# Two tiles in turn for the raw rotary rows, and a softmax that works in place in the probability tiles

## The chip, the cores and the metric

The kernel runs on one core of a Trainium2 chip. The metric is the device time of one execution in microseconds (us). Five engines work at the same time, each through its own list of instructions in order: PE (TensorE, matrix products into PSUM), DVE (VectorE), ACT (ScalarE), POOL (GpSimd) and SP, which here only issues DMAs. They are tied to each other by semaphores: an instruction can wait until a counter has reached a value, and raises another when it is done.

## The reference, cut to what matters

One transformer layer on `x` of 64 sequences, 64 tokens, 512 features: a conditioning product, latent attention with rotary positions, a residual, then a product with a per-sequence adapter and a mixture of four experts. The change touches the attention alone:

```python
h = x @ WA + bA                                   # x here is the conditioned input
kv_lat, q_lat = jnp.split(h, 2, axis=-1)
kRt = _rope(h @ WB + bB, 0)                       # 64 rotary key features, shared by the heads
qRt = _rope(h @ WC + bC, 0)                       # 16 heads x 64 rotary query features
...
scores = jnp.einsum('bhqd,bhkd->bhqk', qf, kf) * dk ** (-0.5)
scores = jnp.where(causal, scores, -jnp.inf)
attn = jax.nn.softmax(scores, axis=-1)
```

`_rope(x)` is `x * cos + rot * sin`, where `rot` swaps the two features of each pair, with a minus sign on the first.

## The kernel before, in words

`absorb_weights` prepares products of weights, `attention` follows, then `routing` and `experts`. In the profile the attention fills the time from 47 us to about 1000 us. It goes through 8 groups g of 8 sequences, each 512 tokens wide. The code is written out by hand for each engine: a part `first` for the start of group 0, and a `body` that is looped over the groups and holds the rest of group g together with the start of group g+1. The order inside an engine's list is the order of the source; nothing is reordered.

**The rotary chain.** The rotary features stand in nine blocks of 128x512 a group: one of keys and eight of queries, u = 0 to 7. A block passes through four engines:

- PE writes the product into one of two PSUM banks, `bank_p[u % 2]` (three matmuls for each of two halves of the latent, L95 to L97).
- ACT adds the bias and writes the block to the tile `raw` (`keys_raw` L500, `q_raw` L507). The profile calls the tile rope_raw.
- POOL multiplies `raw` by the cosines into `q_rope` (`q_cos` L424; for keys `keys_cos` L416, twice as long, into `kblk`).
- DVE (`turn` L629) issues a one-element memset that only carries waits (L633), swaps the pairs of `raw` into `swapped` (shuffle L634) and multiplies by the sines (L638). Then `queries_rope` adds the result to `q_rope` (L657), or `keys_rope` adds it to `kblk` (two halves, L649).

There is one `raw`. ACT may write block u only when DVE has swapped and POOL has multiplied the block before it (waits on `swap_ev` and `cos_ev`, L505 and L506). PE uses a bank again only when ACT has emptied it (`raw_ev`, L851 and L859).

The chain runs twice for each group. I call the two places **the front** (blocks keys, 0, 1, 2, 3 of group g+1, written into the end of group g's body) and **the middle** (blocks 4 to 7 of group g, in the first third of its body). PE's list there is as follows, with Q(u) the product of block u, wz the output projection of an attention step into `bank_o`, and KA(h) the absorbed keys of head h:

- front: Q0, wz, Q1, wz, Q2, wz, Q3, wz, KA0, KA1, then the first product of wz of step 6. KA0 waits for block 2 to be in `raw`, KA1 for block 3.
- middle: Q4, two wz, Q5, two wz, Q6, two wz, Q7, two wz, a transpose, KA8, KA9, mix of step 2, then the first product of wz of step 1. KA8 waits for block 6, KA9 for block 7.

The wz of a step overwrites `bank_o`, so its first product waits for `x2_ev` (L921): DVE must have added the last result to the residual rows (`x2_tile`, L699). The places of `x2_tile` in DVE's list matter below. In the middle it is queries_rope(4), the sum of step 3, queries_rope(5), queries_rope(6), **x2_tile(0)**, queries_rope(7). In the front it is keys_rope, queries_rope(0), queries_rope(1), **x2_tile(5)**, queries_rope(2), queries_rope(3).

POOL's list in the middle is cosines 4, cosines 5, `gated` of step 3 (L431, which waits for DVE's reciprocal), `residual_bias` (L437), cosines 6, cosines 7. In the front it is the keys' cosines, then 0 to 3. ACT's list holds the copies to `raw` in a row, behind the exponential of step 3 in the middle.

**The softmax.** Each group has 8 steps. `less_max` on DVE scales and masks the scores from PSUM into `score` (L675), takes the maximum (L680) and subtracts it (L682); ACT takes the exponential of `score` into `prob[i % 2]` (L516); `softmax_sum` sums it (L688), and POOL multiplies `prob` by the reciprocal (L431). Step n of `less_max` waits for the exponential of step n-1 (`exp_ev`), as there is one `score`. The sum of step n-1, which waits for that same exponential, stands ahead of it in DVE's list in every case.

Of the kernel before, what the change touches and what calls it, by code (L numbers as in the profile page):

```python
# [26 lines left out]
ALU = mybir.AluOpType  # L27
ACT = mybir.ActivationFunctionType
AX = mybir.AxisListType.X
# [285 lines left out]
def attention(nc, K, A, W, out):  # L315

    with ExitStack() as ctx:
        def sb(name, shape, dt=F32):
            return ctx.enter_context(nc.sbuf_tensor(name, shape, dt))
# [19 lines left out]
        lat_h, lat_l = sb("lat_h", [P, 2, GT], F32R), sb("lat_l", [P, 2, GT], F32R)  # L339
        kv_tok = sb("kv_tok", [P, GB, L])  # L340
        q_rope = sb("q_rope", [P, UB, GT])
        raw, swapped = sb("rope_raw", [P, GT]), sb("rope_swapped", [P, GT])
        lat_bias = (raw, swapped)
        bias_sel = swapped[0:NSUB, :].rearrange("n (b d) -> n b d", b=GB)
        score = sb("score", [P, HB, C])
        prob = sb("prob", [P, 2, HB, C])
        rmax, rsum, rinv = sb("rmax", [P, HB]), sb("rsum", [P, HB]), sb("rinv", [P, HB])
        wait_here = sb("wait_here", [1, 1])
# [56 lines left out]
        @block.gpsimd  # L405
        def _(pool):
            def bias_rows(g):
                pool.wait_ge(S["rope_done"], g * NR)
                nc.gpsimd.tensor_tensor(bias_sel[:, :, :],
                                        K["sel"][:, bass.ds(g * GB, GB)].unsqueeze(2).to_broadcast([NSUB, GB, C]),  # L410
                                        K["fside"][:, :].unsqueeze(1).to_broadcast([NSUB, GB, C]),
                                        ALU.mult).then_inc(S["bias_sel_ready"], 1)

            def keys_cos(g):
                pool.wait_ge(S["raw_ev"], g * NR + 1)
                nc.gpsimd.tensor_tensor(kblk[:, :, :, :],  # L416
                                        raw[:, :].rearrange("p (b t) -> p b t", b=GB).unsqueeze(2).to_broadcast([P, GB, 2, C]),
                                        K.parts["cosk"].rearrange("p (h t) -> p h t", h=2).unsqueeze(1).to_broadcast(
                                            [P, GB, 2, C]), ALU.mult).then_inc(S["cos_ev"], 1)

            def q_cos(g, u):
                pool.wait_ge(S["raw_ev"], g * NR + u + 2)
                cos = K.parts["cosq"][:, u * C:(u + 1) * C]
                nc.gpsimd.tensor_tensor(q_rope[:, u % UB, :].rearrange("p (b t) -> p b t", b=GB),  # L424
                                        raw[:, :].rearrange("p (b t) -> p b t", b=GB),
                                        cos.unsqueeze(1).to_broadcast([P, GB, C]), ALU.mult).then_inc(S["cos_ev"], 1)


            def gated(g, i):
                pool.wait_ge(S["inv_ev"], g * STEPS + i + 1)  # L430
                nc.gpsimd.tensor_tensor(prob[:, i % 2, :, :], prob[:, i % 2, :, :],  # L431
                                        rinv[:, :].unsqueeze(2).to_broadcast([P, HB, C]),
                                        ALU.mult).then_inc(S["prob_ev"], 1)

            def residual_bias(g, t):
                pool.wait_ge(xres_in[t], g * 16 + 16)
                nc.gpsimd.tensor_tensor(x_res[:, t, :], x_res[:, t, :], K["bZ"][:, :],  # L437
                                        ALU.add).then_inc(S["xres_biased"], 1)

            def project_front(g):  # L440
                keys_cos(g)
                for u in range(UB):
                    q_cos(g, u)

            def first():
                bias_rows(0)
                project_front(0)
                gated(0, 0)
                gated(0, 1)

            def body(g, more):
                gated(g, 2)
                residual_bias(g, 0)
                q_cos(g, 4)
                q_cos(g, 5)
                gated(g, 3)
                residual_bias(g, 1)
                q_cos(g, 6)
                q_cos(g, 7)
                residual_bias(g, 2)  # L460
                gated(g, 4)
                if more:
                    bias_rows(g + 1)
                residual_bias(g, 3)
                gated(g, 5)
                gated(g, 6)
                gated(g, 7)
                if more:
                    project_front(g + 1)
                    gated(g + 1, 0)  # L470
                    gated(g + 1, 1)

            over_groups(pool, first, body)

        @block.scalar
        def _(act):
# [20 lines left out]
            def keys_raw(g):  # L497
                act.wait_ge(S["lat_ev"], g * 2 + 2)
                act.wait_ge(S["keys_mm"], g + 1)
                nc.scalar.activation(raw[:, :], bank_p[1][:, :], ACT.Identity, bias=K["bB"][:, 0:1]  # L500
                                     ).then_inc(S["raw_ev"], 1)

            def q_raw(g, u):
                act.wait_ge(S["qr_mm"], g * NU + u + 1)
                act.wait_ge(S["swap_ev"], g * NR + u + 1)  # L505
                act.wait_ge(S["cos_ev"], g * NR + u + 1)  # L506
                nc.scalar.activation(raw[:, :], bank_p[u % 2][:, :], ACT.Identity, bias=K["bC"][:, u:u + 1]  # L507
                                     ).then_inc(S["raw_ev"], 1)

            def keys_absorbed(g, h):  # L510
# [2 lines left out]

            def exps(g, i):
                act.wait_ge(S["sub_ev"], g * STEPS + i + 1)
                nc.scalar.activation(prob[:, i % 2, :, :], score[:, :, :], ACT.Exp).then_inc(S["exp_ev"], 1)  # L516

            def prob_transposed(g, i):
                act.wait_ge(S["pt_mm"], g * STEPS + i + 1)
# [87 lines left out]
        def _(dve):  # L607
# [18 lines left out]
                nc.vector.tensor_tensor(lat_l[:, i, :], lat32[i], lat_h[:, i, :].bitcast(F32),  # L626
                                        ALU.subtract).then_inc(S["lat_lo"], 1)

            def turn(r, sin):  # L629

                dve.wait_ge(S["raw_ev"], r + 1)
                dve.wait_ge(S["rope_done"], r)
                nc.vector.memset(wait_here[:, :], 0.0)  # L633
                nc.vector.stream_shuffle(swapped[:, :], raw[:, :], [i ^ 1 for i in range(32)]  # L634
                                         ).then_inc(S["swap_ev"], 1)
                dve.wait_ge(S["swap_ev"], r + 1)
                v = swapped[:, :].rearrange("p (b t) -> p b t", b=GB)
                nc.vector.tensor_tensor(v, v, sin.unsqueeze(1).to_broadcast([P, GB, C]), ALU.mult  # L638
                                        ).then_inc(S["sin_ev"], 1)
                dve.wait_ge(S["sin_ev"], r + 1)  # L640

            def keys_rope(g):
                r = g * NR
                dve.wait_ge(S["lat_ev"], g * 2 + 2)
                turn(r, K.parts["sink"])
                dve.wait_ge(S["cos_ev"], r + 1)
                for h in range(2):
                    rows = slice(h * DR, (h + 1) * DR)
                    last = nc.vector.tensor_tensor(kblk[rows, :, h, :], kblk[rows, :, h, :],  # L649
                                                   swapped[rows, :].rearrange("p (b t) -> p b t", b=GB), ALU.add)  # L650
                last.then_inc(S["rope_done"], 1)

            def queries_rope(g, u):
                r = g * NR + 1 + u
                turn(r, K.parts["sinq"][:, u * C:(u + 1) * C])
                dve.wait_ge(S["cos_ev"], r + 1)
                nc.vector.tensor_tensor(q_rope[:, u % UB, :], q_rope[:, u % UB, :], swapped[:, :], ALU.add  # L657
                                        ).then_inc(S["rope_done"], 1)
# [8 lines left out]
            def per_head(row):  # L667
                return row[:, :].unsqueeze(2).to_broadcast([P, HB, C])

            def less_max(g, i, first=False):  # L670
                n = g * STEPS + i + 1
                dve.wait_ge(S["s_mm"], n)
                if not first:
                    dve.wait_ge(S["exp_ev"], n - 1)
                nc.vector.scalar_tensor_tensor(out=score[:, :, :],  # L675
                                               in0=bank_s[i % 2][:, :].rearrange("p (h t) -> p h t", h=HB), scalar=SCALE,
                                               in1=K.parts["mask"].unsqueeze(1).to_broadcast([P, HB, C]),
                                               op0=ALU.mult, op1=ALU.add).then_inc(S["score_ev"], 1)
                dve.wait_ge(S["score_ev"], n)
                nc.vector.tensor_reduce(rmax[:, :], score[:, :, :], AX, ALU.max).then_inc(S["max_ev"], 1)  # L680
                dve.wait_ge(S["max_ev"], n)
                nc.vector.tensor_tensor(score[:, :, :], score[:, :, :], per_head(rmax),  # L682
                                        ALU.subtract).then_inc(S["sub_ev"], 1)

            def softmax_sum(g, i, first=False):
                n = g * STEPS + i + 1
# [21 lines left out]
            def first():  # L708
# [7 lines left out]
                keys_rope(0)  # L716
                for u in range(UB):
                    queries_rope(0, u)
                less_max(0, 0, first=True)
                softmax_sum(0, 0, first=True)  # L720
                less_max(0, 1)
                softmax_sum(0, 1)
# [1310 lines left out]
```

## Time and profile before

| | us |
|---|---|
| median of 3 runs | 1977.47 |
| lowest and highest of the runs | 1977.43 and 1979.97 |
| the profiled execution, its time | 1983.41 |
| the profiled execution, its span (first to last instruction) | 1981.5 |
| of the span: PE busy | 1849.3 |
| of the span: DVE, POOL, ACT busy | 927.4, 716.0, 627.8 |

The durations used below come from the profiled execution. Its time is 1.9 us more than its span and 5.9 us more than the median of the runs. A group is what lies between one KA9 and the next, some 115 to 117 us. The granted clock is the share of TensorE's full 2.4 GHz that the chip gave: 1.00 is full speed and 0.50 is 1.2 GHz.

### The profile page before, as it was taken

To read this page: it belongs to the slowest core of one execution; us is meant where nothing else is said; L and a number is where in the kernel's file an instruction comes from. 1 tells how busy PE (TensorE), PEld (TensorE's weight loads), DVE (VectorE), ACT (ScalarE), POOL (GpSimd) and SP (SyncE) were. 2 spreads that over 40 slices of the span, in tenths; PEclk is the share of its full clock that TensorE was granted. 3 is DMA by queue.
4 is the path that set the end of the run, shared out by engine and by line. 5 is a ranking of instruction groups with operands and counts; after the bars stand their busy time and mean duration, and the time that the engine had idled before them with its cause. 6 is when DMAs were issued, how large, how long until landed. Compare 5 with 4: busy or idle time off the path is not lost. (4 is left out here: it accounts for less than half of the span.)

```text
span 1981.5 us, 26865 instructions
## 1 busy us (share of the span) xinstructions
PE 1849.3 (93%) x9384; PEld 1434.4 (72%) x9384; DVE 927.4 (47%) x1589; ACT 627.8 (32%) x1088; POOL 716.0 (36%) x524
## 2 busy tenths in 40 slices
PE   6799999999999999999979997999999999999996
PEld 4577676767777676767767775878787878787875
DVE  4566656656665665666422585233323232223321
ACT  4333333333333333333223212333333333333331
POOL 1232222223221222322100013666656574757563
PEclk9999999999999999999989997999999999999998
DMA  7000101001010100101043214223303330422011
GB/s 251 22 1 17 48 5 58 0 26 37 16 48 5 58 0 26 37 16 48 11 111 106 75 64 145 79 41 127 65 21 81 110 64 0 123 89 42 2 20 22
DMA packets 69028, 104.88 MB, mean 53 GB/s; under 512 B 12288, under 2 KB 29440, under 8 KB 68992
## 3 DMA queue, kind: packets, MB, share of 16 engines
q1 hardware_dynamic: 49408, 77.70, 11.8%
q0 software_dynamic: 7168, 16.78, 4.6%
q10 hardware_dynamic: 12416, 9.92, 1.6%
q8 instruction: 23, 0.38, 0.1%
q14 instruction: 13, 0.11, 0.0%
HBM read 79.21 MB, written 25.17 MB: 53 GB/s over the span
## 5 line engine op out<-in xcount | busy, mean ns | idle before, releaser
L1843 DVE CAST hh<-hid 128x512 fp32r<-128x512 f32 x128 | 77.3, 604 | 474.7 <-ACT hid L1788 474.5
L1718 POOL TENSOR_TENSOR w1l<-w_raw,w1h 128x512 fp32r<-128x512 f32 x112 | 179.5, 1603 | 163.6 <-ACT w1h L1780 151.7
L431 POOL TENSOR_TENSOR prob<-prob,rinv 128x512 f32<-128x512 f32 x64 | 66.7, 1043 | 469.6 <-DVE rinv L692 469.6
L95 PE MATMUL e_h<-xh,w1h 128*128 (+1 forms) x512 | 202.8, 396 | 14.7 <-POOL w1l L1718 13.3
L95 PE MATMUL bank_o<-Mh,mix_h 128*128 128x512 f32 x512 | 213.3, 417 | 2.3 <-DVE mix_l L663 1.4
L97 PE MATMUL bank_o<-Mh,mix_l 128*128 128x512 f32 x512 | 203.8, 398 | 0.0
L96 PE MATMUL bank_o<-Ml,mix_h 128*128 128x512 f32 x512 | 203.5, 397 | 0.0
L95 PE MATMUL e_y<-w2h,hh 128*128 128x512 f32 x512 | 200.3, 391 | 1.6 <-DVE hl L1845 1.6
L96 PE MATMUL e_h<-xl,w1h 128*128 (+1 forms) x512 | 201.4, 393 | 0.0
L97 PE MATMUL e_h<-xh,w1l 128*128 (+1 forms) x512 | 201.2, 393 | 0.0
L97 PE MATMUL e_y<-w2h,hl 128*128 128x512 f32 x512 | 199.4, 389 | 0.0
L96 PE MATMUL e_y<-w2l,hh 128*128 128x512 f32 x512 | 199.3, 389 | 0.0
L1723 POOL TENSOR_TENSOR w2l<-w_raw,w2h 128x512 fp32r<-128x512 f32 x112 | 151.0, 1348 | 52.3 <-ACT w2h L1784 52.3
L1788 ACT ACTIVATE hid<-e_h 128x512 f32<-128x512 f32 x128 | 76.7, 599 | 264.7 <-PE e_h L97 264.7
L424 POOL TENSOR_TENSOR q_rope<-rope_raw,table_attend 128x512 f32<-128x512 f32 x64 | 102.6, 1603 | 80.4 <-ACT rope_raw L507 80.4
L1784 ACT CAST w2h<-w_raw 128x512 fp32r<-128x512 f32 x112 | 69.7, 622 | 179.9 <-PE e_y L97 179.9
L95 PEld LDWEIGHTS e_h<-xh,w1h 128*128 128x128 f32 x512 | 97.3, 190 | 38.1 <-POOL w1l L1718 16.3
L95 PEld LDWEIGHTS bank_o<-Mh,mix_h 128*128 128x128 f32 x512 | 97.9, 191 | 30.9 <-issue 10.7
L97 PEld LDWEIGHTS bank_o<-Mh,mix_l 128*128 128x128 f32 x512 | 97.4, 190 | 23.3
L95 PEld LDWEIGHTS e_y<-w2h,hh 128*128 128x128 f32 x512 | 96.1, 188 | 22.9 <-DVE hl L1845 3.3
L97 PEld LDWEIGHTS e_h<-xh,w1l 128*128 128x128 f32 x512 | 97.3, 190 | 20.5
L96 PEld LDWEIGHTS bank_o<-Ml,mix_h 128*128 128x128 f32 x512 | 98.3, 192 | 19.0
(278 smaller groups left out, 3561.3 us busy)
## 6 DMA issues: line engine op xcount, KB each, us to landing
w_raw<-in_W_dram SPq DMA_DIRECT2D x56, 512.0 KB, 4.2
stage<-in_x_dram SPq DMA_DIRECT2D x8, 1024.0 KB, 6.3
x_res<-in_x_dram SPq DMA_DIRECT2D x32, 256.0 KB, 2.7
out_dram<-x_res SPq DMA_DIRECT2D x32, 256.0 KB, 2.0
flat_dram<-flat_sb ACTq DMA_DIRECT2D x32, 256.0 KB, 2.0
rows<-out_dram SPq DMA_DIRECT2D x4, 1024.0 KB, 5.1
x_odd<-out_dram SPq DMA_DIRECT2D x4, 1024.0 KB, 6.0
stage<-in_W_dram SPq DMA_DIRECT2D x8, 512.0 KB, 5.8
```

Source lines behind the costliest of these rows:

```text
L95: nc.tensor.matmul(out, ah, bh, start=start and n == 0, stop=False)
L96: nc.tensor.matmul(out, ah, bl, start=False, stop=False)
L97: last = nc.tensor.matmul(out, al, bh, start=False, stop=stop and n == len(pairs) - 1)
L424: nc.gpsimd.tensor_tensor(q_rope[:, u % UB, :].rearrange("p (b t) -> p b t", b=GB), raw[:, :].rearrange("p (b t) -> p b t", b=GB), cos.uns ...
L431: nc.gpsimd.tensor_tensor(prob[:, i % 2, :, :], prob[:, i % 2, :, :], rinv[:, :].unsqueeze(2).to_broadcast([P, HB, C]), ALU.mult).then_inc ...
L1718: nc.gpsimd.tensor_tensor(w1l[:, k, :, :], w1_at(pair, chunk), w1h[:, k, :, :].bitcast(F32), ALU.subtract).then_inc(S["w1_lo"], 1)
L1723: nc.gpsimd.tensor_tensor(w2l[:, k, :], w2_at(pair, chunk), w2h[:, k, :].bitcast(F32), ALU.subtract).then_inc(S["w2_lo"], 1)
L1784: nc.scalar.copy(w2h[:, k, :], w2_at(pair, chunk)).then_inc(S["w2_hi"], 1)
L1788: nc.scalar.activation(hid[:, k, :], bank_h[k][:, :], ACT.Gelu).then_inc(S["h_act"], 1)
L1843: nc.vector.tensor_copy(hh[:, k, :], hid[:, k, :]).then_inc(S["h_hi"], 1)
```

## The change

`raw` becomes two tiles. Block u of the queries uses `raw[u % 2]`, and the keys use `raw[1]`. ACT's copy of block u now waits for the swap and the cosines of the block two before it, and the copy of block 0 has no such wait at all. `score` is gone: `less_max` writes its three results to the half of `prob` that the exponential then overwrites in place, and no longer waits for `exp_ev`. The tiles together take the same space. Every engine's list holds the same work in the same order as before; only waits and the tiles read and written differ.

```diff
-        raw, swapped = sb("rope_raw", [P, GT]), sb("rope_swapped", [P, GT])
-        lat_bias = (raw, swapped)
+        raw = [sb(f"rope_raw{k}", [P, GT]) for k in range(2)]
+        swapped = sb("rope_swapped", [P, GT])
+        lat_bias = (raw[0], swapped)
...
-        score = sb("score", [P, HB, C])
...
             def keys_raw(g):
                 act.wait_ge(S["lat_ev"], g * 2 + 2)
                 act.wait_ge(S["keys_mm"], g + 1)
-                nc.scalar.activation(raw[:, :], bank_p[1][:, :], ACT.Identity, bias=K["bB"][:, 0:1]
+                nc.scalar.activation(raw[1][:, :], bank_p[1][:, :], ACT.Identity, bias=K["bB"][:, 0:1]
...
             def q_raw(g, u):
                 act.wait_ge(S["qr_mm"], g * NU + u + 1)
-                act.wait_ge(S["swap_ev"], g * NR + u + 1)
-                act.wait_ge(S["cos_ev"], g * NR + u + 1)
-                nc.scalar.activation(raw[:, :], bank_p[u % 2][:, :], ACT.Identity, bias=K["bC"][:, u:u + 1]
+                if u:
+                    act.wait_ge(S["swap_ev"], g * NR + u)
+                    act.wait_ge(S["cos_ev"], g * NR + u)
+                nc.scalar.activation(raw[u % 2][:, :], bank_p[u % 2][:, :], ACT.Identity, bias=K["bC"][:, u:u + 1]
...
-                nc.scalar.activation(prob[:, i % 2, :, :], score[:, :, :], ACT.Exp).then_inc(S["exp_ev"], 1)
+                nc.scalar.activation(prob[:, i % 2, :, :], prob[:, i % 2, :, :], ACT.Exp).then_inc(S["exp_ev"], 1)
...
+                row = prob[:, i % 2, :, :]
                 dve.wait_ge(S["s_mm"], n)
-                if not first:
-                    dve.wait_ge(S["exp_ev"], n - 1)
-                nc.vector.scalar_tensor_tensor(out=score[:, :, :],
-                                               in0=bank_s[i % 2][:, :].rearrange("p (h t) -> p h t", h=HB), scalar=SCALE,
+                nc.vector.scalar_tensor_tensor(out=row, in0=bank_s[i % 2][:, :].rearrange("p (h t) -> p h t", h=HB),
...
-                nc.vector.tensor_reduce(rmax[:, :], score[:, :, :], AX, ALU.max).then_inc(S["max_ev"], 1)
+                nc.vector.tensor_reduce(rmax[:, :], row, AX, ALU.max).then_inc(S["max_ev"], 1)
...
-                nc.vector.tensor_tensor(score[:, :, :], score[:, :, :], per_head(rmax),
-                                        ALU.subtract).then_inc(S["sub_ev"], 1)
+                nc.vector.tensor_tensor(row, row, per_head(rmax), ALU.subtract).then_inc(S["sub_ev"], 1)
```

The shuffle in `turn` and the two cosine products read `raw[1]` or `raw[u % 2]` in the same way.

## Rows read from the trace of the kernel before

**Rows 1.** The page's first part: busy us, share of the span, instructions.

```profile
PE 1849.3 (93%) x9384; PEld 1434.4 (72%) x9384; DVE 927.4 (47%) x1589; ACT 627.8 (32%) x1088; POOL 716.0 (36%) x524
```

**Rows 2.** PE's waits, whole span: us in total, times, longest us.

```profile
PE bank_p L95 <- ACT rope_raw L507: 42.7, 32, 2.2
```

**Rows 3.** Timeline, middle of group 1: start, us, operation xcount [idle before <-releaser].

```profile
224.84 1.30 POOL L424 TENSOR_TENSOR q_rope<-rope_raw,table_attend 128x512 f32<-128x512 f32 x1 [3.54 <-ACT rope_raw L507]
...
225.73 0.96 DVE L638 TENSOR_TENSOR rope_swapped<-rope_swapped,table_attend 128x512 f32<-128x512 f32 x1
...
226.72 0.69 DVE L657 TENSOR_TENSOR q_rope<-q_rope,rope_swapped 128x512 f32<-128x512 f32 x1
...
227.00 1.57 POOL L424 TENSOR_TENSOR q_rope<-rope_raw,table_attend 128x512 f32<-128x512 f32 x1 [0.86 <-ACT rope_raw L507]
...
228.28 0.74 DVE L634 STREAM_SHUFFLE rope_swapped<-rope_raw 128x512 f32<-128x512 f32 x1
...
229.54 1.73 POOL L437 TENSOR_TENSOR x_res<-x_res,bZ 128x512 f32<-128x512 f32 x1
```

**Rows 4.** The timeline goes on, up to the first wz of step 1.

```profile
230.16 1.66 DVE L657 TENSOR_TENSOR q_rope<-q_rope,rope_swapped 128x512 f32<-128x512 f32 x1
...
231.23 1.71 POOL L424 TENSOR_TENSOR q_rope<-rope_raw,table_attend 128x512 f32<-128x512 f32 x1
...
233.77 0.50 PE L95 MATMUL bank_p<-lat_h,Ah 128*128 128x512 f32 x1 [1.94 <-ACT rope_raw L507]
...
234.13 0.68 DVE L699 TENSOR_TENSOR x_res<-bank_o,x_res 128x512 f32<-128x512 f32 x1
...
235.73 0.50 PE L95 MATMUL bank_o<-Mh,mix_h 128*128 128x512 f32 x1
```

**Rows 5.** Timeline, front of group 2.

```profile
293.00 2.21 DVE L638 TENSOR_TENSOR rope_swapped<-rope_swapped,table_attend 128x512 f32<-128x512 f32 x1
...
295.24 2.39 DVE L649 TENSOR_TENSOR k_blocks<-k_blocks,rope_swapped 64x512 f32<-64x512 f32 x2
...
295.50 1.57 POOL L424 TENSOR_TENSOR q_rope<-rope_raw,table_attend 128x512 f32<-128x512 f32 x1 [0.86 <-ACT rope_raw L507]
...
298.65 0.69 ACT L507 ACTIVATE rope_raw<-bank_p,bC 128x512 f32<-128x512 f32 x1 [3.23 <-DVE rope_swapped L634]
...
299.38 0.69 DVE L657 TENSOR_TENSOR q_rope<-q_rope,rope_swapped 128x512 f32<-128x512 f32 x1
...
300.24 0.75 DVE L634 STREAM_SHUFFLE rope_swapped<-rope_raw 128x512 f32<-128x512 f32 x1
...
302.42 0.68 DVE L699 TENSOR_TENSOR x_res<-bank_o,x_res 128x512 f32<-128x512 f32 x1
...
304.52 0.50 PE L95 MATMUL bank_p<-lat_h,Ah 128*128 128x512 f32 x1 [1.50 <-ACT rope_raw L507]
```

**Rows 6.** Timeline, PE in the front of group 1: KA1 and what follows it.

```profile
189.24 0.51 PE L95 MATMUL bank_p<-lat_h,Ah 128*128 128x512 f32 x1 [0.88 <-ACT rope_raw L507]
...
190.05 0.39 PE L95 MATMUL bank_o<-Mh,mix_h 128*128 128x512 f32 x1
```

**Rows 7.** Timeline, end of the attention: a wz product that waits for `x2_tile`.

```profile
974.13 0.69 DVE L699 TENSOR_TENSOR x_res<-bank_o,x_res 128x512 f32<-128x512 f32 x1 [2.22 <-PE bank_o L97]
...
974.97 0.48 PE L95 MATMUL bank_o<-Mh,mix_h 128*128 128x512 f32 x1 [0.44 <-DVE x_res L699]
```

**Rows 8.** Timeline, PE in the front of group 0: its KA1.

```profile
78.81 0.50 PE L95 MATMUL bank_p<-lat_h,Ah 128*128 128x512 f32 x1 [1.45 <-ACT rope_raw L507]
```

**Rows 9.** Busy us (instructions) by stretch; after POOL the granted clock, DMA share, GB/s.

```profile
117.20:120.40 3.20, 3.20 (x11) 1.69 (x10) 3.13 (x6) 1.42 (x4) 2.24 (x2) 0.50 0.01 3
305.00:308.20 3.20, 3.20 (x9) 2.46 (x8) 2.42 (x6) 0.59 (x1) 1.34 (x1) 0.50 0.24 74
233.77:350.57 116.80, 111.28 (x617) 82.63 (x617) 71.06 (x128) 38.85 (x68) 29.94 (x22) 0.99 0.08 27
350.57:465.74 115.17, 109.65 (x616) 81.49 (x616) 71.08 (x128) 38.83 (x68) 29.97 (x22) 1.00 0.08 27
```

More of the change, by code:

```diff
@@ L416, in keys_cos @@
                 nc.gpsimd.tensor_tensor(kblk[:, :, :, :],
-                                        raw[:, :].rearrange("p (b t) -> p b t", b=GB).unsqueeze(2).to_broadcast([P, GB, 2, C]),
+                                        raw[1][:, :].rearrange("p (b t) -> p b t", b=GB).unsqueeze(2).to_broadcast([P, GB, 2, C]),
                                         K.parts["cosk"].rearrange("p (h t) -> p h t", h=2).unsqueeze(1).to_broadcast(
@@ L424, in q_cos @@
                 nc.gpsimd.tensor_tensor(q_rope[:, u % UB, :].rearrange("p (b t) -> p b t", b=GB),
-                                        raw[:, :].rearrange("p (b t) -> p b t", b=GB),
+                                        raw[u % 2][:, :].rearrange("p (b t) -> p b t", b=GB),
                                         cos.unsqueeze(1).to_broadcast([P, GB, C]), ALU.mult).then_inc(S["cos_ev"], 1)
@@ L627, in latent_lo, with turn @@
                                         ALU.subtract).then_inc(S["lat_lo"], 1)
-            def turn(r, sin):
+            def turn(r, k, sin):
                 dve.wait_ge(S["raw_ev"], r + 1)
@@ L633, in turn @@
                 nc.vector.memset(wait_here[:, :], 0.0)
-                nc.vector.stream_shuffle(swapped[:, :], raw[:, :], [i ^ 1 for i in range(32)]
+                nc.vector.stream_shuffle(swapped[:, :], raw[k][:, :], [i ^ 1 for i in range(32)]
                                          ).then_inc(S["swap_ev"], 1)
@@ L644, in keys_rope @@
                 dve.wait_ge(S["lat_ev"], g * 2 + 2)
-                turn(r, K.parts["sink"])
+                turn(r, 1, K.parts["sink"])
                 dve.wait_ge(S["cos_ev"], r + 1)
@@ L654, in queries_rope @@
                 r = g * NR + 1 + u
-                turn(r, K.parts["sinq"][:, u * C:(u + 1) * C])
+                turn(r, u % 2, K.parts["sinq"][:, u * C:(u + 1) * C])
                 dve.wait_ge(S["cos_ev"], r + 1)
@@ L668, in per_head, with less_max @@
                 return row[:, :].unsqueeze(2).to_broadcast([P, HB, C])
-            def less_max(g, i, first=False):
+            def less_max(g, i):
                 n = g * STEPS + i + 1
+                row = prob[:, i % 2, :, :]
                 dve.wait_ge(S["s_mm"], n)
-                if not first:
-                    dve.wait_ge(S["exp_ev"], n - 1)
-                nc.vector.scalar_tensor_tensor(out=score[:, :, :],
-                                               in0=bank_s[i % 2][:, :].rearrange("p (h t) -> p h t", h=HB), scalar=SCALE,
-                                               in1=K.parts["mask"].unsqueeze(1).to_broadcast([P, HB, C]),
+                nc.vector.scalar_tensor_tensor(out=row, in0=bank_s[i % 2][:, :].rearrange("p (h t) -> p h t", h=HB),
+                                               scalar=SCALE, in1=K.parts["mask"].unsqueeze(1).to_broadcast([P, HB, C]),
                                                op0=ALU.mult, op1=ALU.add).then_inc(S["score_ev"], 1)
                 dve.wait_ge(S["score_ev"], n)
-                nc.vector.tensor_reduce(rmax[:, :], score[:, :, :], AX, ALU.max).then_inc(S["max_ev"], 1)
+                nc.vector.tensor_reduce(rmax[:, :], row, AX, ALU.max).then_inc(S["max_ev"], 1)
                 dve.wait_ge(S["max_ev"], n)
-                nc.vector.tensor_tensor(score[:, :, :], score[:, :, :], per_head(rmax),
-                                        ALU.subtract).then_inc(S["sub_ev"], 1)
+                nc.vector.tensor_tensor(row, row, per_head(rmax), ALU.subtract).then_inc(S["sub_ev"], 1)
             def softmax_sum(g, i, first=False):
@@ L718, in first @@
                     queries_rope(0, u)
-                less_max(0, 0, first=True)
+                less_max(0, 0)
                 softmax_sum(0, 0, first=True)
```

## The prediction

> **What bounds the kernel now.** I read the busy shares first: PE is busy 93% of the span and no other engine over half [rows 1]. So the time is PE's list, and the change can only alter the waits in it. The list of waits by engine comes next. The largest wait of PE is for ACT's copy to the raw rotary tile, 42.7 us in 32 waits [rows 2]. The softmax does not appear among PE's waits. The timeline then shows who makes each copy late. In the middle, KA9 has stood still for 1.94 us for block 7 [rows 4]. In the front, the copy of block 1 starts at 298.65, released by DVE's shuffle, and KA1 is held for 1.50 us [rows 5]. What the reader should look for in these rows is how long the same operation takes. L638, L657 and L649 on DVE read two SBUF tiles and take 0.69 us when POOL is quiet, but 0.96, 1.66 and 2.21 us when POOL is at work [rows 3 to 5].
>
> **How DVE and POOL block each other.** Block 4's cosines end at 226.14 and L638, begun during them, ends at 226.69, which is 0.55 later. The bias row L437 ends at 231.27 and L657, begun during it, ends at 231.82, again 0.55 later [rows 3, 4]. So DVE's two-input operation stands until POOL's ends. The other way round, the cosines begun at 231.23 end 1.12 after L657, and those begun at 227.00 end 1.16 after it, against 1.30 for an undisturbed one [rows 3, 4]. My two rules for this kernel are thus: **blocked DVE operation ends 0.55 after POOL's, blocked POOL cosine or bias operation ends 1.15 after DVE's**, and the one already waiting goes ahead of the one issued later. L437 was waiting at 229.54, and L657 at 230.16 had to let it pass [rows 3, 4].
>
> **The removed wait of the softmax.** It costs nothing today: the sum of step n-1 stands ahead of `less_max(n)` in DVE's list and waits for the same exponential. In place or not, the instructions have the same sizes. I put this part at 0; a few tens of ns in 64 steps on an engine with slack would not reach PE either way.
>
> **The middle, worked through.** ACT can now copy block 5 right behind block 4 (ready about 225.5, one copy of 0.69 after the start of block 4's cosines), block 6 as soon as its product is there, and block 7 after the shuffle of block 5. Block 4's steps up to 226.69 stay. Then:
> - POOL no longer waits for block 5. It has been ready since 226.14, goes next, and its cosines end at 226.69 + 1.15 = 227.84. Before, they began at 227.00, after L657 had got in [rows 3].
> - L657 of block 4 is therefore blocked and ends at 228.39 instead of 227.41: 0.98 lost.
> - Block 5's shuffle began 0.87 after L657's end [rows 3], so now at 229.26, ending at 230.00. The copy of block 7 is done at 230.7. KA9, which could follow KA8 at 231.8 (233.77 less 1.94), has **no wait left**: 1.94 us gained.
> - L437 began 2.13 after that L657's end, as `gated` ended [rows 3], so now at 230.52. L638 of block 5 ends at 231.10, L437 at 232.25, L657 of block 5 at 232.80.
> - Block 6: cosines end at 233.95, L638 at 234.50. Before, block 7's cosines came after L657 of block 6. Now block 7 is ready and waiting, so they go first, until 235.65, and L657 of block 6 ends at 236.20: once more 1 us lost.
> - x2_tile(0) stands behind it and starts 0.08 before its end, at 236.12 instead of 234.13 [rows 4].
> - The first wz of step 1 may start 0.84 after x2_tile's start [rows 7]: **236.96 instead of 235.73** [rows 4]. PE would be there at 233.8 (235.73 less 1.94) and stands for some 3.2 us.
>
> So each middle loses 1.23 us: the wait for block 7 is replaced by a longer one for x2_tile(0). Eight middles: **+9.8 us**. From below, with POOL's earlier cosines costing DVE nothing, x2_tile stays at 234.13, wz starts at 234.97, and a middle gains 0.76.
>
> **The front, worked through.** Keys' L638 ends at 295.21 [rows 5]. Block 0 is ready by then, as nothing holds its copy, and its cosines end at 296.36. The first half of L649 ends at 296.91, block 1's cosines at 298.06, the second half at 298.61 instead of 297.63 [rows 5]. The copy that block 0's shuffle released began 1.02 after L649 [rows 5]. Now that is block 2's, so it runs from 299.63 to 300.32. L657 of block 0 ended 2.44 after L649 [rows 5]: 301.05. Block 2's cosines end at 302.20, L638 of block 1 at 302.75. Block 1's shuffle ended 3.36 after L649 [rows 5], so the copy of block 3 is done 4.08 after it, at 302.69. KA1 starts at 302.74 instead of 304.52. Before, wz came 0.81 after KA1 [rows 6], nominally at 305.33. Now it also needs x2_tile(5), behind L657 of block 1. That L657 is issued at 302.79, and block 3's cosines at 302.77. The two are within 0.03:
> - POOL first: cosines until 304.07, L657 until 304.62, x2_tile from 304.54, wz at 305.38: **0.0 gained**.
> - DVE first: L657 until 303.48, x2_tile from 303.40, wz at 304.24: **1.09 gained**.
> - From below, with no new blocking: copy of block 3 after the shuffle's end at 300.99, KA1 at 301.76, x2_tile as before at 302.42, wz at 303.26, 2.07 gained.
>
> I take the first, since POOL's request is the earlier one. Seven fronts: **0.0 us**, ends 0 and -14.5. On this tie the Trainium skill says (SBUF — State Buffer, Who interferes with whom) that issue order decides who blocks. That names POOL by the order worked out above; a wrong order of 0.03 would move the sum by 7 x 1.09 = 7.6 us. The front of group 0 has no x2_tile. Its KA1 moves like the other, by 302.74 - 304.52 = -1.78, from 78.81 [rows 8]: **-1.8 us**.
>
> **The clock.** After a stall the granted clock is at 0.50 for a stretch. This follows 3 of the 8 middles (first: 117.2) and 5 of the 7 fronts (first of full cost: 305.0) [rows 9]. A group with one such stretch takes 116.80, one with none 115.17 [rows 9]: **1.6 us each**. A front has some 3.3 us of waits within 7 us. The new middle has about 3.2 us in one piece, so I give it the front's share: 8 x 5/7 = 5.7 stretches instead of 3, +2.7 x 1.6 = **+4.4 us**. The ends are 0 and, with all fifteen places hit, 7 x 1.6 = +11.2.
>
> **Sum.** 9.8 + 0.0 - 1.8 + 4.4 = +12.4 us on the profiled execution (1983.4 to 1995.8, span 1981.5 to 1993.9). On the median of the runs it gives 1977.5 + 12.4 = **1990 us**. Behind the two places nothing else that the change delays is waited for soon: blocks 2 and 3 of a front are needed by the next group's scores, behind six more KA and six wz products, and block 7 of a middle by step 4's scores, later still.
>
> **Rivals.**
> - *DVE first in the fronts.* For it: L657 has won by 0.04 elsewhere. Against: here it is second. 12.4 - 7.6 = +4.8, **1982 us**.
> - *Double buffering pays.* The new tile takes DVE's and POOL's turns off the chain without new blocking: 7 x -2.07, 8 x -0.76, and the first front at -2.7 (78.81 to 76.1) make -23.3, and up to four stretches of low clock fewer -6.4; between them **1951 us**. For it: PE waits 42.7 us for this tile [rows 2]. Against: DVE's list is already full from the first shuffle on, and POOL's turns move onto it. It decides the case if POOL's cosines do not get in ahead of L657.
> - *The clock falls at every place.* 9.8 - 1.8 + 11.2 = +19.2, **1997 us**. For it: a middle's wait grows from 1.9 to 3.2 us. The Trainium skill warns of this (TensorE: Matmul & The Clock Gate, HAM oscillation): a wait that recurs in each tile makes the engine pay the clock's step each time. No row here has a single attention stall of that length, so the chance rests on the fronts.
> - *Nothing moves.* Gains of fronts and losses of middles cancel, without more low clock: 9.8 - 7.6 - 1.8 = +0.4, **1978 us**.
>
> **How the numbers follow.** Chances: forecast 0.40, DVE first 0.20, pays 0.17, clock at every place 0.15, nothing 0.08. "Faster" and "slower" mean by over 0.2% (4 us), about what can be told from no change: faster 0.17. Same takes the last and the lower half of DVE first, 0.18; slower is the rest, 0.65. The range runs from just below "nothing moves" to just above the clock rival, 1975 to 2000, and leaves "pays" out.
>
> **What would show it.** In the timeline of the middle: block 5's cosines start as block 4's end, L657 of block 4 takes 1.7 instead of 0.69, KA9 has no wait, and the first wz of step 1 waits about 3.2 us for x2_tile. In PE's waits: the 42.7 us fall to about 20, and a new row for x_res L699 has 25 us (8 x 3.2) plus up to 13 (7 x 1.8). The distance of one KA9 to the next grows by 1.2 us, or 1.2 plus a multiple of 1.6. I am wrong if L657 of block 4 still takes 0.69, or if wz waits for something else.

## The result, and the profile after

| | before | changed |
|---|---|---|
| median, us | 1977.47 (1976.43 to 1984.36, 5 runs) | 1991.51 (1989.88 to 1992.95, 4 runs) |
| ratio to before | | 1.0061, 95% interval 1.0045 to 1.0078 |
| again, beside the experiments below | 1980.02 (17 runs) | 1991.51 (6 runs), ratio 1.0053, 1.0040 to 1.0066 |
| profiled execution: time, span | 1983.41, 1981.5 | 1989.88, 1987.9 |

The changed kernel is slower by 0.5 to 0.6%, 11.5 to 14 us. One more execution of it took 2104.89 us at a mean granted clock of 0.84, where the others had 0.97, and is left out. The two profiled executions are only 6.5 us apart, because that of before is one of its longer ones. Later readings therefore use stretches that can be compared, not the two spans.

PE's waits in the changed kernel, whole span (total us, times, longest); the first rows answer to [rows 2]:

```profile
PE bank_o L95 <- DVE x_res L697: 26.2, 14, 3.2
PE bank_p L95 <- ACT rope_raw L508: 19.5, 17, 2.8
```

The 42.7 us for the raw tile have become 19.5, and a wait of 26.2 us for `x2_tile` has appeared. Before, PE waited 0.9 us for `x2_tile`, in two places at the end of the attention. So the sum of the two rows went from 43.6 to 45.7, 2 us more. That alone does not explain 11.5 us or more.

The middle of group 1 in the timeline, answering to [rows 3, 4]. L639 and L658 are before's L638 and L657, L697 is its L699:

```profile
221.98 2.99 POOL L424 TENSOR_TENSOR q_rope<-rope_raw,table_attend 128x512 f32<-128x512 f32 x2 [3.54 <-ACT rope_raw L508]
...
222.86 0.96 DVE L639 TENSOR_TENSOR rope_swapped<-rope_swapped,table_attend 128x512 f32<-128x512 f32 x1
...
223.85 1.67 DVE L658 TENSOR_TENSOR q_rope<-q_rope,rope_swapped 128x512 f32<-128x512 f32 x1
...
226.43 1.04 POOL L431 TENSOR_TENSOR prob<-prob,rinv 128x512 f32<-128x512 f32 x1 [1.47 <-DVE rinv L690]
227.43 1.75 POOL L437 TENSOR_TENSOR x_res<-x_res,bZ 128x512 f32<-128x512 f32 x1
...
228.06 1.67 DVE L658 TENSOR_TENSOR q_rope<-q_rope,rope_swapped 128x512 f32<-128x512 f32 x1
...
229.14 3.40 POOL L424 TENSOR_TENSOR q_rope<-rope_raw,table_attend 128x512 f32<-128x512 f32 x2
...
231.44 1.64 DVE L658 TENSOR_TENSOR q_rope<-q_rope,rope_swapped 128x512 f32<-128x512 f32 x1
...
233.01 0.68 DVE L697 TENSOR_TENSOR x_res<-bank_o,x_res 128x512 f32<-128x512 f32 x1
...
233.83 0.77 PE L95 MATMUL bank_o<-Mh,mix_h 128*128 128x512 f32 x1 [3.15 <-DVE x_res L697]
```

POOL's cosines now run in pairs (x2, 2.99 and 3.40 us), and each second one falls on an L658: the adds of blocks 4 and 6 (223.85 and 231.44) take 1.67 and 1.64 us where 0.69 stood before. The add of block 5 (228.06) was blocked before too, 1.66 us. DVE reaches `x2_tile(0)` late, and PE stands for 3.15 us.

The front of group 2, answering to [rows 5]:

```profile
295.88 3.37 DVE L650 TENSOR_TENSOR k_blocks<-k_blocks,rope_swapped 64x512 f32<-64x512 f32 x2
...
303.42 0.69 DVE L658 TENSOR_TENSOR q_rope<-q_rope,rope_swapped 128x512 f32<-128x512 f32 x1
...
303.46 1.79 POOL L424 TENSOR_TENSOR q_rope<-rope_raw,table_attend 128x512 f32<-128x512 f32 x1 [0.69 <-ACT rope_raw L508]
```

PE in the same front:

```profile
290.47 0.40 PE L95 MATMUL bank_p<-lat_h,WBh 128*128 128x512 f32 x1
...
300.97 0.50 PE L95 MATMUL bank_p<-lat_h,Ah 128*128 128x512 f32 x1 [0.61 <-ACT rope_raw L508]
...
303.44 0.50 PE L95 MATMUL bank_p<-lat_h,Ah 128*128 128x512 f32 x1 [1.50 <-ACT rope_raw L508]
...
304.86 0.47 PE L95 MATMUL bank_o<-Mh,mix_h 128*128 128x512 f32 x1 [0.46 <-DVE x_res L697]
```

The keys' adds (L650, before's L649) take 3.37 instead of 2.39. Of the near tie, DVE won by 0.04 (303.42 against 303.46), so `x2_tile(5)` is hardly late: 0.46 us of wait.

**A measure for a group.** From the first matmul of the keys' block in one front to that in the next, PE's work is the same in both kernels. The rows are of the kind of [rows 9]: the stretch, its length, the busy time (and count) of PE, PEld, DVE, ACT and POOL, then the granted clock, the DMA share and GB/s. First before: six groups in one piece, then one group alone.

```profile
174.22:873.55 699.33, 666.97 (x3697) 495.04 (x3696) 426.44 (x763) 233.01 (x403) 179.69 (x132) 0.99 0.08 27
406.57:521.75 115.18, 109.66 (x617) 81.49 (x616) 71.09 (x128) 38.85 (x68) 29.97 (x22) 1.00 0.08 27
```

And for the changed kernel, six groups and then the longest kind of group:

```profile
172.52:878.16 705.64, 671.23 (x3698) 500.42 (x3696) 436.54 (x763) 233.80 (x403) 185.66 (x132) 0.97 0.08 27
407.17:525.95 118.78, 113.42 (x617) 84.39 (x616) 72.75 (x128) 38.96 (x68) 30.95 (x22) 0.96 0.08 26
```

A group at full clock took 115.18 us before; its mean over six was 116.56 (699.33 / 6). The changed kernel's mean is 117.61, and its clock over the six groups is 0.97 instead of 0.99. It has no group at full clock: the first takes 117.95 us, and the others alternate between 116.7 and 118.8. So the traces alone do not say how much of the 1.05 us a group is wait and how much is clock. The experiments below separate them.

### The profile page after: what moved, and what is told of

Read it like the earlier page. It is cut to its first block and busy times, and to the rows that moved or that the text cites. A ratio compares the mean times of both kernels' runs of the same rounds, so it can differ in the third digit from the quotient of the medians.

```text
span 1987.9 us, 26787 instructions
## 1 busy us (share of the span) xinstructions
PE 1855.8 (93%) x9384; PEld 1443.2 (73%) x9384; DVE 934.6 (47%) x1589; ACT 629.2 (32%) x1088; POOL 724.5 (36%) x524
## 5 line engine op out<-in xcount | busy, mean ns | idle before, releaser
L1841 DVE CAST hh<-hid 128x512 fp32r<-128x512 f32 x128 | 71.8, 561 | 482.9 <-ACT hid L1786 482.9
L95 PE MATMUL bank_o<-Mh,mix_h 128*128 128x512 f32 x512 | 215.0, 420 | 27.7 <-DVE x_res L697 26.2
L424 POOL TENSOR_TENSOR q_rope<-rope_raw,table_attend 128x512 f32<-128x512 f32 x64 | 107.2, 1689 | 50.7 <-ACT rope_raw L508 50.6
L96 PEld LDWEIGHTS e_h<-xl,w1h 128*128 128x128 f32 x512 | 98.2, 192 | 20.3
```

Of the source, the lines that this page charges most:

```text
L95: nc.tensor.matmul(out, ah, bh, start=start and n == 0, stop=False)
L96: nc.tensor.matmul(out, ah, bl, start=False, stop=False)
L1841: nc.vector.tensor_copy(hh[:, k, :], hid[:, k, :]).then_inc(S["h_hi"], 1)
```

## The experiments

I call **the port** whatever it is that DVE's two-input operations and POOL's operations share. The rows show it only by its effect, that one stands until the other ends.

Theory: the rotary copies are early enough now, but POOL's earlier cosines keep DVE from the port, `x2_tile(0)` is late, and after the longer wait the clock is low. Rivals: the in-place softmax costs something; the fronts lose, not the middles; the wait counts and the clock does not. Each line of the table stands against 1979.8 to 1980.1 us of the kernel before, which ran beside them. "Six groups" is the measure above, from each kernel's profile. The last column is the mean granted clock over all executions of that kernel; the kernel before has 0.975 to 0.976. What it is worth can be estimated from two executions of the kernel before, 1976.85 us at 0.978 and 1985.69 us at 0.972: about 1.5 us for each 0.001.

| kernel | median, us | ratio, 95% interval | six groups, us | clock |
|---|---|---|---|---|
| in place only | 1980.05 | 0.9999 (0.9988 to 1.0009) | 699.02 | 0.976 |
| double in middles only | 1988.80 | 1.0047 (1.0033 to 1.0061) | 704.35 | 0.974 |
| double in fronts only | 1976.09 | 0.9987 (0.9978 to 0.9996) | 693.18 | 0.973 |
| changed, POOL held in middles | 1976.17 | 0.9981 (0.9972 to 0.9990) | 697.01 | 0.968 |
| changed, x2_tile earlier | 1955.39 | 0.9866 (0.9851 to 0.9881) | 678.69 | 0.974 |
| before, x2_tile earlier | 1981.22 | 1.0009 (0.9997 to 1.0021) | 700.11 | 0.975 |
| changed, x2_tile earlier, POOL held everywhere | 1962.55 | 0.9905 (0.9891 to 0.9920) | 683.42 | 0.971 |
| changed again | 1991.51 | 1.0053 (1.0040 to 1.0066) | 707.07 | 0.967 |
| changed, middles filled | 1979.68 | 0.9997 (0.9988 to 1.0006) | 695.55 | 0.974 |
| changed, middles and fronts filled | 1971.34 | 0.9954 (0.9939 to 0.9969) | 691.56 | 0.981 |
| changed, x2_tile earlier, fronts filled | 1948.21 | 0.9836 (0.9821 to 0.9851) | 672.03 | 0.979 |
| before, fronts filled | 1978.60 | 0.9996 (0.9987 to 1.0005) | 696.56 | 0.976 |

**The softmax in place alone.** The kernel before, with `score` replaced by the rows of `prob` and without the wait for `exp_ev`, as in the diff of the change.

> The kernel before with the softmax in place alone: no score tile, no wait for the exponential, one raw rotary tile as before. Port theory (all of the loss comes from POOL's cosines getting ahead of L657): as before, 1977 us within 3 us, PE waits 42 to 43 us for the raw tile. Rival, that the softmax in place costs something: part or all of the 14 us, 1982 to 1991 us, and the exponential or the three DVE steps of a softmax longer than their 0.63 and 0.69 us.

Measured 1980.05 us, ratio 0.9999. PE's wait for the raw tile is 43.9 us in 33 waits. The grouped rows of ACT and of DVE in this kernel, 93 to 910 us (busy us, mean ns of one | idle before):

```profile
L515 ACT ACTIVATE prob<-prob 128x512 f32<-128x512 f32 x57 | 36.0, 632 | 96.6 <-DVE prob L679 95.9
...
L679 DVE TENSOR_TENSOR prob<-prob,rmax 128x512 f32<-128x512 f32 x57 | 39.4, 692 | 2.0
```

The exponential takes 632 ns and the subtraction 692 ns, as before. This part of the change is worth nothing in time. It gives the space of `score` to the second raw tile.

**The two places apart.** In the changed kernel, the copies of one place wait for the block just before, as they did before the change:

```diff
             def q_raw(g, u):
                 act.wait_ge(S["qr_mm"], g * NU + u + 1)
-                if u:
-                    act.wait_ge(S["swap_ev"], g * NR + u)
-                    act.wait_ge(S["cos_ev"], g * NR + u)
+                back = 0 if u >= UB else 1
+                act.wait_ge(S["swap_ev"], g * NR + u + back)
+                act.wait_ge(S["cos_ev"], g * NR + u + back)
```

> The changed kernel, but in the fronts (blocks 0 to 3) ACT waits for the block just before, as it did before the change; only the middles use the two tiles in turn. Port theory: the first wz of step 1 waits 3.15 us for x2_tile(0) in each middle as in the changed kernel, and the fronts are those of before, so the fronts' gain of some 1 us each is gone: 1991.5 + 8 = 1999 us, at least 1993. Rival, that the loss sits in the fronts: 1977 us or less.

The kernel for the fronts has 0 and 1 the other way round, and keeps `if u:`, so that the copy of block 0 has no such wait.

> The changed kernel, but in the middles (blocks 4 to 7) ACT waits for the block just before; only the fronts use the two tiles in turn. Port theory: middles as before (KA9 waits 1.94 us, no wait for x2_tile(0)), fronts about 1 us shorter each: 1977.5 - 1.8 - 7 = 1969 us. Rival, that the loss sits in the fronts or in anything both places share: 1985 us or more.

Measured 1988.8 and 1976.1 us. The signs are the theory's and against the rival: middles lose, fronts gain. The sizes are not. The fronts were to give 8 to 9 us against before (1969) and give 3.7; the middles were to cost 13 to 19 and cost 9. A group of the middles-only kernel at full clock, then a group of the fronts-only kernel with one stretch at 0.50:

```profile
413.21:529.37 116.16, 109.53 (x617) 81.49 (x616) 71.83 (x128) 38.94 (x68) 30.75 (x22) 1.00 0.08 27
```

```profile
233.08:348.82 115.74, 111.06 (x616) 82.63 (x616) 71.92 (x128) 38.82 (x68) 30.20 (x22) 0.99 0.08 27
```

The first is 0.98 us longer than before's 115.18, and that is the pure price of a middle. The second, less 1.6 for its stretch, is 114.1: 1.0 less, the pure gain of a front.

The clock explains the sizes in part. Eight middles at 0.98 are 7.8 of the 9 us. The expectation had added what the changed kernel loses by its clock, and in this kernel little of that is there: the six groups hold 7.4 us of it (704.35 - 6 x 116.16), before's hold 8.2 (699.33 - 6 x 115.18), although each of its middles has the wait of 3.15 us. In the fronts-only kernel the six groups are 6.2 us shorter than before's, but the medians differ by only 3.7. The profiled execution of before is 3.6 us above the median of 1979.8 and this one is at its median, and the mean clock is 0.973 against 0.975, some 3 us by the estimate above. So a part of the fronts' gain went to the clock; the runs do not show how much more closely than that.

**POOL held back in the middles.** In the changed kernel, one wait more:

```diff
             def q_cos(g, u):
                 pool.wait_ge(S["raw_ev"], g * NR + u + 2)
+                if u in (5, 7):
+                    pool.wait_ge(S["rope_done"], g * NR + u + 1)
```

> The changed kernel with one wait more on POOL: the cosines of blocks 5 and 7 start only when DVE has added block 4 and block 6. ACT's copies are as early as in the changed kernel. Port theory: L657 of blocks 4 and 6 is back at 0.69 us, x2_tile(0) comes 2 us earlier, the wait for it falls from 3.15 to about 1.2 us in each middle; 8 x 2 = 16 us less, 1975 us, or 1970 with fewer stretches of low clock. Rival, that the loss has another cause than the order at the port: 1991 us or more, since the edit only adds a wait.

Measured 1976.17 us, 15 us less by a wait that was only added. The middle of group 1 in this kernel (L660 is the add, L426 the cosines, L699 x2_tile):

```profile
222.64 0.69 DVE L660 TENSOR_TENSOR q_rope<-q_rope,rope_swapped 128x512 f32<-128x512 f32 x1
...
223.48 1.29 POOL L426 TENSOR_TENSOR q_rope<-rope_raw,table_attend 128x512 f32<-128x512 f32 x1 [1.42 <-DVE q_rope L660]
...
229.73 0.69 DVE L660 TENSOR_TENSOR q_rope<-q_rope,rope_swapped 128x512 f32<-128x512 f32 x1
```

PE at the end of that middle:

```profile
231.17 0.51 PE L95 MATMUL bank_o<-Mh,mix_h 128*128 128x512 f32 x1 [1.71 <-DVE x_res L699]
```

The adds of blocks 4 and 6 are back at 0.69, and the wait for `x2_tile(0)` has fallen from 3.15 to 1.71 (1.2 was expected). The order at the port is shown as the cause of the lateness. The clock has hardly a part in these 15 us: its mean is 0.968, and 0.967 in the changed kernel.

**x2_tile(0) one place earlier.** In DVE's list of the changed kernel, and then of the kernel before:

```diff
                 queries_rope(g, 5)
-                queries_rope(g, 6)
                 x2_tile(g, 0)
+                queries_rope(g, 6)
                 queries_rope(g, 7)
```

> The changed kernel with x2_tile(0) one place earlier in DVE's list, ahead of queries_rope(6). Port theory with the wait for x2_tile as the price: the 3.15 us in front of the first wz of step 1 are gone in the seven looped middles and 1.5 us in the last, 23.5 us less, and the stretches of low clock behind the middles with them (up to 8 x 1.6 us): 1958 to 1968 us. L657 of block 4 still takes 1.67 us. Rival, that the clock or the timing of later stages made the difference: 1985 us or more.

> The kernel before with the same move of x2_tile(0). With one raw tile the copy of block 7 waits for the shuffle of block 6, which x2_tile now pushes 0.7 us back, past the end of its cosines: KA9 waits some 0.4 us longer, 8 x 0.4 = 3 us more, 1980 us. So the move helps only where the raw tile is doubled. Rival, that the place of x2_tile was a flaw in itself: 1970 us or less.

Measured 1955.39 and 1981.22 us. With two raw tiles the move is worth 36 us against the changed kernel, and ends 3 us below the range expected; with one it is worth nothing. In the first kernel the add of block 4 still takes 1.67 us and PE waits nowhere in the middles. The two edits need each other: one takes away PE's wait for block 7, the other its wait for x2_tile(0). A part of the expectation for the second kernel failed. Its wait for KA9 is 2.01 us, 0.07 more than before and not 0.4, since the shuffle of block 6 slipped past the end of its cosines by less than I had worked out.

**POOL held back everywhere.** The kernel with x2_tile earlier, and the wait of `q_cos` for u in (1, 3, 5, 7).

> The changed kernel with x2_tile(0) ahead of queries_rope(6) and the cosines of blocks 1, 3, 5 and 7 held back until DVE has added the block before. Port theory: as the kernel with x2_tile earlier, and in the fronts L649 falls from 3.37 to about 2.4 us, so KA0 and KA1 come up to 1 us earlier: 5 to 7 us less than that kernel, 1953 to 1962 us. Rival, that holding POOL back only moves the wait to the copies: the same as the kernel with x2_tile earlier or slower.

Measured 1962.55 us, 7 us slower than the same kernel without it: the expectation failed. The front of group 2 in it:

```profile
286.37 2.36 DVE L652 TENSOR_TENSOR k_blocks<-k_blocks,rope_swapped 64x512 f32<-64x512 f32 x2
...
291.26 2.96 POOL L426 TENSOR_TENSOR q_rope<-rope_raw,table_attend 128x512 f32<-128x512 f32 x2 [3.78 <-DVE q_rope L660]
...
293.12 1.65 DVE L660 TENSOR_TENSOR q_rope<-q_rope,rope_swapped 128x512 f32<-128x512 f32 x1
```

L652 did fall to 2.36. But the cosines of block 1 were held until block 0 was added, ran straight into those of block 2 (x2, 2.96 us), and blocked the add of block 1 just ahead of `x2_tile(5)`. The blocking had moved from the keys' adds to the add that PE's first wz waits behind. A front's waits of 0.61, 1.50 and 0.46 us became 1.82 and 1.18 us, 0.43 more, or 3 us in seven fronts. The rest of the 7 us is not traced; the mean clock is lower as well, 0.971 against 0.974.

**Filling PE's waits.** This tests the clock by itself. Matmuls of no use go where PE would wait, into the bank of the transposes, which is free there. DVE, POOL and ACT do what they did. The last two calls of `fill` stand in the second kernel only.

```diff
+            def fill(n):
+                for _ in range(n):
+                    nc.tensor.matmul(bank_t[:, :], W["WCh"][:, 0, 0:P], lat_h[:, 0, :], start=True, stop=True)
...
                 mix(g, 2)
+                fill(13 if more else 6)
                 for k in range(6):
                     wz(g, 1, (k, ))
...
+                    fill(2)
                     keys_absorbed(g + 1, 0)
+                    fill(6)
                     keys_absorbed(g + 1, 1)
```

> The changed kernel once more, unedited, on the chip of the runs that follow, to have a level to compare them with: 1991 us, 0.6% over the kernel before.

> The changed kernel with 13 matmuls of no use (128x512, 0.23 us each, 6 in the last group) into a free PSUM bank behind the mix of step 2, where PE otherwise waits 3.15 us for x2_tile(0). All results stay as they are. Theory that the low clock behind that wait is a third part of the loss: the wait is filled, the stretches at 0.50 behind the middles (6 of 7 looped ones in the changed kernel, three of them double) vanish, and the time falls by 8 to 12 us to 1980 us, although PE does 3 us more work in each middle. Rival, that only the wait itself counts: 1991 us or more.

> As the kernel with filled middles, and 2 and 6 such matmuls ahead of KA0 and KA1 in the seven fronts, where PE waits 0.61 and 1.50 us. Clock theory: the stretches behind the fronts vanish too (3 of 7), 3 to 5 us less again, 1976 us. Rival: no change against the kernel with filled middles, or slower.

Measured 1991.51, 1979.68 and 1971.34 us. PE executes 13 matmuls more in each looped middle, and in the second kernel 8 more in each looped front, and the kernel is 11.8 and then 20.2 us faster. The second step is 8.3 us and not the 3 to 5 expected. With the middles filled, a stretch at 0.50 stood behind 6 of 7 fronts, where the changed kernel has one behind 3. The six groups of the kernel with both filled:

```profile
171.95:863.51 691.56, 686.03 (x3823) 512.65 (x3822) 437.09 (x763) 233.59 (x403) 186.12 (x132) 1.00 0.08 27
```

The clock is 1.00 throughout and a group takes 115.26 us (691.56 / 6). That is the changed kernel's group without low clock, and it is before's 115.18 within 0.1. **With the clock out of the way the change neither gains nor loses in a group**: the fronts' gain and the middles' loss cancel. The loss of the real kernel is the clock. Its group is 117.6 to 117.8 long, 2.4 to 2.6 of it at the clock's cost, where before paid 1.4 (116.56 - 115.18). The mean clock of all executions says the same: 0.967 against 0.975, about 12 us by the estimate above. And the middles' long waits alone did not bring this loss, as the middles-only kernel shows; it came with both places changed.

**The two best edits together.** x2_tile(0) earlier, and the fronts filled with 2 and 6.

> The changed kernel with x2_tile(0) ahead of queries_rope(6) (1955 us) and the fronts filled with 2 and 6 matmuls of no use. That kernel had one stretch at 0.50 behind each of six fronts. Clock theory: they vanish, 6 x 1.6 = 10 us less, 1946 us. Rival, that they do not depend on PE's waits: 1955 us or more.

Measured 1948.21 us, ratio 0.9836: 1.6% better than before and 2.2% better than the changed kernel. Its group is 112.0 us at full clock:

```profile
170.33:842.36 672.03, 666.54 (x3745) 498.33 (x3744) 442.32 (x763) 233.63 (x403) 183.42 (x132) 1.00 0.08 28
```

**The kernel before with filled fronts.** Its PE waits ahead of Q3, KA0 and KA1 filled with 6, 1 and 6 matmuls. The middles could not be filled in the same way, since the bank is still being read there.

> The kernel before with 6, 1 and 6 matmuls of no use ahead of Q3, KA0 and KA1 in the seven looped fronts, where PE waits 1.56, 0.29 and 1.50 us. All results stay as they are. Clock theory: its stretches at 0.50 behind fronts (5 of 7) go, 5 x 1.6 = 8 us less, 1972 us, about the 1971 us of the changed kernel with filled waits; so with the low clock away the change is worth nothing either way. Rival, that the changed kernel with filled waits is truly the faster one: 1977 us or more here.

Measured 1978.60 us, ratio 0.9996: not the 1972 of the clock theory, and not clearly its rival, which said 1977 or more because of an advantage in waits. The trace decides between them:

```profile
173.49:870.05 696.56, 680.91 (x3775) 506.02 (x3774) 426.67 (x763) 233.01 (x403) 179.83 (x132) 0.99 0.08 27
```

```profile
288.99:405.82 116.83, 114.25 (x631) 84.85 (x630) 71.08 (x128) 38.83 (x68) 29.95 (x22) 0.99 0.08 27
405.82:521.06 115.24, 112.68 (x631) 83.88 (x629) 71.08 (x128) 38.85 (x68) 29.98 (x22) 1.00 0.08 27
```

A group at full clock is still 115.24, so there is no difference in waits to before or to the filled changed kernel. But half of the groups still have a stretch, now behind the unfilled middles, with their 1.9 us of wait. The six groups are only 2.8 us shorter than before's. Filling one place did not remove its share of the low clock; in this kernel, as in the one with filled middles, stretches stood at the other.

## Why the prediction was right, point by point

- **What bounds the kernel, and the softmax at 0:** held. PE's list is the time, and the in-place softmax alone measured 0.9999.
- **The two rules of the port** (0.55 and 1.15): held. Worked out for the changed middle were adds of blocks 4 and 6 that each lose 1 us, no wait at KA9, and some 3.2 us ahead of the first wz of step 1. The trace has 1.67 and 1.64 for the adds, no wait at KA9, and 3.15. The experiment that only holds POOL back shows the cause. In the last middle, which is not looped, the wait is only 1.46.
- **The middle, +1.23 each:** right in sign, a little too large. The middles-only kernel has 0.98 (116.16 against 115.18 at full clock), so 8 middles are +7.8, not +9.8. The wait itself was forecast within 0.05. Most of the 0.25 comes from one step of the working. It let L437 begin 2.13 after the add of block 4; in the changed kernel it begins 1.91 after (227.43 - 225.52). Before, `gated` stood behind the cosines of block 5 in POOL's list, which end at 228.57 [rows 3]; now these are long done and it waits for DVE's reciprocal alone.
- **The front, 0.0 each: this step failed.** I gave the near tie to POOL by 0.02 us. DVE had it by 0.04, and each front gained 1.1: first matmul of the keys to wz takes 14.39 (290.47 to 304.86), where before it took 15.5 (289.83 to 305.33, the nominal time worked out in the prediction). Seven fronts gave -7.7 instead of 0. That this moved the sum by 7.6 was on record as the case "DVE first", at 0.20. A tie inside the scatter of the durations should have been left even.
- **The first front, -1.8:** in the changed kernel its KA1 comes 12.9 us after the keys' first matmul (76.58 - 63.64), 14.7 before (78.81 - 64.14): -1.7. PE in the changed kernel's first front:

```profile
63.64 0.50 PE L95 MATMUL bank_p<-lat_h,WBh 128*128 128x512 f32 x1 [2.23 <-DVE lat_l L627]
...
76.58 0.79 PE L95 MATMUL bank_p<-lat_h,Ah 128*128 128x512 f32 x1 [1.38 <-ACT rope_raw L508]
```

- **The clock, +4.4: the second term that was mis-sized.** I gave the middles the fronts' share of stretches and left the fronts alone. In the profiled execution 6 of the 8 changed middles have one, three of them a double one, and 3 of the 7 fronts have one; in the repeat it is 7 middles and 4 fronts. The clock's cost per group went from 1.4 to 2.4 us, and to 2.6 in the repeat: +7 to +8.4 in seven groups.
- **The sum.** Worked out again with what was measured: middles +7.8, fronts -7.7, first front -1.7, clock +7 to +8.4 in the looped groups, +1.6 for one stretch more behind the first front (a double one there). That makes +7.0 to +8.4. The repeat measured +11.5. The remaining 3 to 4.5 us are a term that the prediction put at nothing. Behind the last residual row both kernels run the same code, but it takes 984.1 us in the profile of before and 986.7 in that of the changed kernel (987.5 in the repeat), at a granted clock of 0.97 and 0.96. Whether that belongs to the change is open: two kernels with one raw tile, before with x2_tile earlier and before with fronts filled, have 988.0 and 986.6 there.
- **So the number was met by luck.** The prediction had 8.0 us from waits (9.8 + 0.0 - 1.8) and 4.4 from the clock. The runs show -1.6 from waits (7.8 - 7.7 - 1.7), +8.6 to +10.0 from the clock in the attention, and 3 to 4.5 outside it. The mechanism of the middle was right, and without it the sign would have been wrong: the case "double buffering pays" had the raw tile's wait right and missed who comes next.

The tile that was short was found correctly by whoever reads [rows 2]. What decides is what DVE and POOL do with the time that an early copy gives them, and what stands behind that in DVE's list.

The last residual row, before and changed:

```profile
997.32 0.69 DVE L699 TENSOR_TENSOR x_res<-bank_o,x_res 128x512 f32<-128x512 f32 x1 [5.36 <-PE bank_o L97]
```

```profile
1001.26 0.69 DVE L697 TENSOR_TENSOR x_res<-bank_o,x_res 128x512 f32<-128x512 f32 x1 [5.35 <-PE bank_o L97]
```

The stretch from there to the end, before and changed, in rows like those of [rows 9]:

```profile
997.32:1981.46 984.14, 921.94 (x4328) 750.61 (x4328) 337.15 (x547) 296.68 (x520) 468.44 (x340) 0.97 0.25 69
```

```profile
1001.26:1987.93 986.67, 925.93 (x4328) 753.80 (x4328) 330.99 (x547) 296.94 (x520) 468.71 (x340) 0.96 0.25 69
```

## What to carry to other kernels

When a buffer is doubled, follow the released work to the resource that it shares with others, and then to the next thing in the order of that engine's list. Here the copy came earlier, POOL's operation took the port ahead of DVE's, and an addition that PE needs stood behind the adds that this delayed. Moving that addition turned a loss of 11.5 us into a gain of 25. And read the granted clock beside the waits: the same schedule, with PE's waits filled by matmuls of no use, was 20 us faster.

## What the runs showed that I had not expected

- Matmuls of no use in PE's waits made the changed kernel 20 us faster (1991.51 to 1971.34), 1.0%. The waits were short: 0.61, 1.50 and 0.46 us in a front, with about 1 us of work between, and 3.15 in a middle. PE's clock over six groups went from 0.97 to 1.00, that is from part of the time at 1.2 GHz to all of it at 2.4.
- The stretches at 0.50 are not additive. Filling before's fronts alone bought 1.5 us, although five stretches stood behind them, and doubling the fronts alone kept 3.7 of 9.4 us (7.7 of the fronts, 1.7 of the first). Doubling the middles alone added none in six groups (7.4 us of clock cost against 8.2), doubling both raised it to 14.1 (705.64 - 6 x 115.26).
- An engine made to wait can speed up the kernel: one more wait on POOL took 15 us off (1991.51 to 1976.17). Added in the middles and the fronts of the kernel with x2_tile earlier, it cost 7 (1955.39 to 1962.55).
- A near tie at the port went to DVE when its add began 0.04 us before POOL's cosines, in the seven looped fronts alike.
